# Sums over sources for ten tiles at a time, a comparison ramp in PSUM, and a prologue in another order

## The reference

```
# layer 0, with x + ... and a layer norm around it
h        = relu(concat(x[src], edge_attr) @ W1.T + b1)
agg      = segment_sum(h @ W2.T + b2, dst)            # per destination
gi, gh   = agg @ Wih.T + bih, x @ Whh.T + bhh         # a GRU cell
r, z     = sigmoid(i_r + h_r), sigmoid(i_z + h_z);  n = tanh(i_n + r * h_n)
x        = layernorm(x + (1 - z) * n + z * x)
# layer 1: a mean over edges, the other way round
agg, deg = segment_sum(x[dst], src), segment_sum(1, src)
x        = layernorm(x + (agg / max(deg, 1)) @ weight + x @ root_weight + bias)
```

## Time and profile before

| | |
|---|---|
| median of 3 runs | 5907.92 us |
| the profiled execution | 5940.19 us, its span 5938.5 us |
| mean granted TensorE clock | 0.832 |
| busy | PE 75%, PEld 64%, DVE 56%, ACT 40%, POOL 55% |
| DMA engines, data moved | 40% to 70% busy in most slices, 998.72 MB |

### The profile page before, as it was taken

One profiled execution on the slowest core, in us unless ns is written; L12 is line 12 of the kernel. 1 busy time (PEld: TensorE's weight loads), 2 busy tenths in 40 slices (PEclk: granted clock), 3 DMA queues, 4 the chain that ended last, 5 costly groups with the idle time before them and its releaser, 6 DMA issues.

```text
span 5938.5 us, 89837 instructions
## 1 busy us (share of the span) xinstructions
PE 4445.1 (75%) x30332; PEld 3789.5 (64%) x30332; DVE 3346.9 (56%) x9964; ACT 2362.5 (40%) x4278; POOL 3250.5 (55%) x3198
## 2 busy tenths in 40 slices
PE   6477777787777777777777877777777777777776
PEld 5366666676666666666666666666666667666654
DVE  5344656565556565655556565655565656565555
ACT  2144343434343434444444434343434343434343
POOL 2466555655555555556555655565555555555520
PEclk8566888787979797988888888888797988788889
DMA  6444657575756565655656565657474656565656
GB/s 182 77 128 128 198 147 199 143 202 145 203 145 194 152 189 160 183 167 173 180 162 190 156 190 148 199 154 200 141 206 144 198 153 192 160 180 163 173 148 178
DMA packets 1017763, 998.72 MB, mean 168 GB/s; under 512 B 204167, under 2 KB 857548, under 8 KB 1016921
## 3 DMA queue, kind: packets, MB, share of 16 engines
q1 hardware_dynamic: 830878, 459.88, 27.8%
q10 hardware_dynamic: 84075, 321.56, 17.1%
q0 software_dynamic: 102352, 211.43, 14.0%
HBM read 655.22 MB, written 337.22 MB: 167 GB/s over the span
## 4 chain that ended last, share of the span: by engine, by line
PE 48%; DVE 17%; another core or an unknown queue 15%; issue 10%; ACT 5%; DVEq 1%; ACTq 0%
PE stream_pse L1163 11%; PE stream_psa L1172 10%; PE stream_psw L1187 9%; PE stream_pse L1155 6%; DVE stream_col L933 5%; PE stream_psw_third L1187 5%; ACT stream_a_sb L848 3%; DVE stream_sums L943 3%; DVE stream_sums L947 2%; DVE stream_row L928 1%; ACT stream_hid L810 1%; DVE stream_yg L911 1%; DVE stream_acc L903 1%; PE stream_psw_third L1211 1%
## 5 line engine op out<-in xcount | busy, mean ns | idle before, releaser
L793 POOL DMA_INDIRECT stream_yg<-y,stream_idx x3125 | 3197.7, 1023 | 2322.7 <-ACT stream_hid L810 1446.9
L848 ACT CAST stream_a_sb<-stream_psa 98x512 f16<-98x512 f32 x3125 | 1772.3, 585 | 2996.1 <-remote 1176.4
L911 DVE TENSOR_TENSOR stream_yg<-stream_pse,stream_yg 128x384 f32<-128x384 f32 x1250 | 611.3, 489 | 1850.1 <-remote 947.1
L1172 PE MATMUL stream_psa<-stream_col,stream_row 128*98 128x256 f16 x6250 | 1292.6, 312 | 439.7 <-ACT stream_a_sb L848 221.8
L1187 PE MATMUL stream_psw<-stream_z,stream_strip 128*128 128x257 f16 x5850 | 930.9, 293 | 407.4 <-DVE stream_sums L947 345.5
L1163 PE MATMUL stream_pse<-w1b,stream_ea 128*128 128x128 f32 x6250 | 1161.7, 327 | 68.5 <-DMA stream_ea<-in_ea_blocks_dram 33.6
L1172 PEld LDWEIGHTS stream_psa<-stream_col,stream_row 128*98 128x98 f16 x6250 | 825.9, 144 | 584.7 <-issue 409.5
L1163 PEld LDWEIGHTS stream_pse<-w1b,stream_ea 128*128 128x128 f32 x6250 | 1006.0, 233 | 117.8 <-issue 91.6
L933 DVE TENSOR_TENSOR stream_col<-iota_lo,stream_twin 128x1536 f16<-128x1536 f16 x1250 | 1020.7, 817 | 0.0
L1187 PEld LDWEIGHTS stream_psw<-stream_z,stream_strip 128*128 128x128 f16 x5850 | 590.9, 104 | 565.5 <-issue 312.9
L1155 PEld LDWEIGHTS stream_pse<-stream_seg,stream_hid 128*128 128x128 f32 x6250 | 855.6, 215 | 1.3
(11 more groups left out here) (202 smaller groups left out, 2053.4 us busy)
## 6 DMA issues: line engine op xcount, KB each, us to landing
A<-stream_a_sb ACTq DMA_DIRECT2D x625, 490.0 KB
stream_strip<-A SPq DMA_DIRECT2D x1862, 160.0 KB
stream_ea<-in_ea_blocks_dram SPq DMA_DIRECT2D x625, 160.0 KB
stream_yg<-y,stream_idx POOLq DMA_INDIRECT x3125
stream_col<-A SPq DMA_DIRECT2D x84, 96.0 KB, 2.5
prologue_xt<-in_xT_dram SPq DMA_DIRECT2D x14, 448.0 KB, 4.9
y<-prologue_ysb SPq DMA_DIRECT2D x14, 448.0 KB, 2.8
stream_yg<-r SPq DMA_DIRECT2D x49, 128.0 KB, 2.5
```

The lines of the kernel that those rows point to most:

```text
L793: nc.gpsimd.indirect_dma_start(out=yg[s.c % 4][:, t, :], out_offset=None, in_=h.y, in_offset=bass.IndirectOffsetOnAxis(ap=idx[s.c // (PH / ...
L848: nc.scalar.copy(a_sb[s.c % AR][0:RW, j, :], psa[BANK[j]][0:RW, :]).then_inc(a_out, 1)
L911: V.tensor_tensor(yg[s.c % 4][:, lo:hi, :], pse[half][:, 0:(hi - lo) * D].rearrange("p (t d) -> p t d", d=D), yg[s.c % 4][:, lo:hi, :], AL ...
L1172: last = nc.tensor.matmul(psa[BANK[j]][0:RW, e * LOS:(e + 1) * LOS], row1[s.c % 2][:, 2 * j + e, :], col1[s.c % 2][:, 2 * j + e, :], start ...
```

## The change

1. **Ten tiles at a time.** The sums over sources are taken once for two phases: a unit is now 10 matmuls over 10 tiles and the same two adds. There are 9 x 98 = 882 units where there were 1764; the matmuls stay 8820. Phase 0 has no units; of the 98 units of each pair, phases 1, 3, ..., 15 take 50 and phases 2, 4, ..., 16 take 48, 2 or 3 a step; phase 17 takes the last 98 alone, 4 at k = 12 and then 5 a step.
2. **Two PSUM banks** for the units and the GRU cell in place of three. A unit waits for the unit two before it; the first of a phase now waits for r as well as z. The strip ring is 4 strips of 10 tiles, no longer 7 of 5. At the end the last 8 tiles come from one strip buffer, loaded three ahead (was six).
3. **The ramp in PSUM.** The third bank holds a copy of `iota_lo`, read as 16-bit numbers, and `rows`, `cols` and `segment_hot` read it there; the keys and the results stay in SBUF.
4. **The prologue.** Two pairs of codes are turned after each of pieces 1 to 7; the one-hots' keys are stored twice side by side, so that the innermost dimension holds two elements one step apart; counts follow pieces 3, 4, 5, 6, and the short chain pieces 8, 9 and 10; weights are loaded at piece 2. SP loads the indices and edge data of the first blocks and POOL gathers blocks 0 to 3 within the prologue, after its 49 windows. The wait for the store of the degrees moves to SP at the stream's start.
5. Some buffers are shared: xb, xtb and rb lie in tt, nn and vb, with one more wait of DVE at k = 9 for the store of r of the phase before.

```diff
-UNITS = {k: 5 for k in range(12, PH)}
-UNITS[PH - 1] = UNITS[PH - 11] = 4
...
+RS = 4
+PAIR = 2 * PT
+UT = ITER // 2 * TS
+def unit_steps(p):
+    if p == 0 or p > ITER - 1:
+        return {}
+    if p == ITER - 1:
+        first, ks = 0, [12, 12, 12, 12] + [k for k in range(13, PH) for _ in range(5)][:TS - 4]
+    elif p % 2:
+        first, ks = 0, [k for k in range(12, PH) for _ in range(3 - k % 2)]
+    else:
+        first, ks = TS * 50 // 98, [k for k in range(13, PH) for _ in range(2 + k % 2)]
...
             def unit(ph, u, first):        # PE
+                if first:
                     pe.wait_ge(z_ready, ph.n(1, 1))
-                if u == 1:
                     pe.wait_ge(r_ready, ph.n(1, 1))
...
-                if u >= 3:
-                    pe.wait_ge(unit_added, ph.n(TS, u - 1))
-                for t in range(PT):
-                    last = nc.tensor.matmul(psw[(u + 2) % 3][:, 0:XC], strip[c % RING][:, t, ...], z[0][:, t, :], ...)
+                if u >= 2:
+                    pe.wait_ge(unit_added, u)
+                for t in range(PAIR):
+                    last = nc.tensor.matmul(psw[u % 2][:, 0:XC], strip[g % RS][:, t, ...], z[g // C % 2][:, t, :], ...)
                 last.then_inc(unit_done, 1)
...
             def unit_first(u):             # DVE
+                dve.wait_ge(unit_done, u + 2)
+                V.tensor_tensor(sums[:, u % TS, :], sums[:, u % TS, :], psw[u % 2][:, 0:P + 1], ALU.add)
...
-        psw = [psw2[:, 0:512], psw2[:, 512:1024], psw_third[:]]
+        psw = [psw2[:, 0:512], psw2[:, 512:1024]]
+        ramp = psi[:, 0:LOS // 2].bitcast(fp16)
...
             def paired(n, groups):
-                return h.iota_lo[:, 0:n].rearrange("p (a b) -> p a b", b=2)...
+                return ramp[:, 0:n].rearrange("p (a b) -> p a b", b=2)...
...
             def load_strip(g, ph, to, at, n):     # SP
+                if g >= RS:
+                    sp.wait_ge(unit_done, 2 * (g - RS) + 3)
...
             # prologue, DVE
-                V.tensor_tensor(oh_hi[q % 2][:], wide(f_hi[:, part], W), tall(h.iota_lo[0:SR, 0:W], SQ), ALU.is_equal)
+                for to, key, n in ((oh_hi[q % 2], f_hi, W), (oh_lo[q % 2], f_lo, P)):
+                    V.tensor_tensor(to as [SR, SQ, n // 2, 2], key[:, part, :] as the same, iota_lo as the same, ALU.is_equal)
...
             # prologue, PE
             for k in range(1, NC):
                 y(k)
-                turn_codes(k - 1)
-                if k % 2 == 1 and 3 <= k <= 9:
-                    count((k - 3) // 2)
-            places()
+                for n in pairs_at(k):          # 2k - 2, 2k - 1
+                    turn_codes(n)
+                if 3 <= k <= 6:
+                    count(k - 3)
+                if k == 8:
+                    halves()
+                if k == 9:
+                    rows_before()
+                if k == 10:
+                    turn_first()
...
             # prologue, POOL, after the 49 windows
+            for k in range(2):
+                pool.wait_ge(y_stored[k], 16 * ((NC + 1 - k) // 2))
+            pool.wait_ge(h.idx_in[0], 16)
+            for c in range(4):
+                for t in range(BT):
+                    nc.gpsimd.indirect_dma_start(out=h.yg[c][:, t, :], ..., in_=h.y, ...)
...
             # prologue, SP: the last line goes, and stands at the stream's start
-            sp.wait_ge(deg_stored, 16)
```

More of the change, by code:

```diff
@@ L233, in pair_tiles, with pairs_at @@
             return [t for t in (2 * n, 2 * n + 1) if t < QS]
+        def pairs_at(k):
+            return [n for n in (2 * k - 2, 2 * k - 1) if 0 <= n < EP]
         def quad_tiles(q):
@@ L1015, in body @@
                         read_places(s, 4 if k is None else min(8, BLOCKS + 1 - s.c))
-                units = units_of(k) if k is not None and ph.p < ITER else []
-                ops = [(f, u) for u in units for f in (unit_first, unit_second)]
+                units = units_of(ph.p, k) if k is not None else []
                 order = []
@@ L1227, in body @@
             def body(s, k=None, ph=None):
-                units = units_of(k) if k is not None and ph.p < ITER else []
+                units = units_of(ph.p, k) if k is not None else []
+                begin = units[0] if units and k == min(STEPS[ph.p]) else None
                 def next_unit():
                     if units:
-                        unit(ph, units.pop(0))
+                        u = units.pop(0)
+                        unit(ph, u, u == begin)
                 pe.wait_ge(ea_in[s.c % 2], s.turn(2, 16))
```

255 lines of the change are left out of this document (144 added, 111 removed).

## The result

The changed kernel takes 6023.13 us (median of 4 runs, 6007.9 to 6035.79), the kernel before in the same set 5907.52 us: ratio 1.0188, 95% interval 1.0171 to 1.0205. The forecast was 5793 us. The profiled execution has a span of 6024.1 us against 5938.5.

The account below looks back on a forecast made before the run. It took PE to bound the steps with units, with a small real wait for DVE; -30 - 125 - 23 + 55 + 8 = -115 us on 5940.19 gave 5825, as a median 5793 us, own range 5660 to 5900.

Parts of the forecast that it names:

- Last section, "loads three strips ahead, 13 us: nothing": Last section: keeps its matmuls and loads three strips ahead, 13 us at its pace a pair; claimed to cost nothing.
- Phase 17, +55: Phase 17: 490 more matmuls in its 20 steps, claimed to add 55 us, bounds +20 and +93.
- "isn't late": SP's queue: the next block's edge data, behind strip loads that wait for units, claimed to come in time.
- Phases 1 to 16, -125 and +8: Steps with units: half the adds saves 0.4 us a step, -125 us; each phase's first unit waiting for r, +8 us.
- the backlog: Steps with units: PE ran 2.0 us behind its record, so some of its recorded waits for adds aren't real.
- Rival 2: Steps with units: PE is truly full, fewer adds return nothing, phase 17 pays its whole 62 us; 5925 us, chance 0.13.
- the first rival: DVE's comparisons: with the ramp in PSUM they fall to one element a cycle, +333 us; 6125 us, chance 0.14.
- the +8 us for the first unit's wait: First unit of a phase: also waits for r, up to some 0.5 us in 17 phases; range 0 to +17.
- Two banks covered by 0.6 to 0.9 us: Units in two PSUM banks: PE's other work outlasts DVE's adds by 0.6 to 0.9 us, hiding the missing third bank.
- Phase 0, -23: Phase 0: without its 490 matmuls it goes at the open blocks' pace, -23 us, bounds 0 and -62.
- Ramp in PSUM, no change: DVE's comparisons: reading the ramp from PSUM leaves their time unchanged; faster POOL gathers, perhaps 266 us, give nothing.
- Prologue, -30: Prologue: block ends 22 us sooner and the first add's wait for gathered rows saves 8; -30 us, bounds -45 and -10.

Follow-up runs that it names:

- e1: Changed kernel with strips loaded seven ahead in the last section, from separate early and late tile buffers; slow chip: 6018.43 us, 1.0124 of the kernel before.
- e2: Changed kernel with SP loading the next block's edge data ahead of the strips; slow chip: 6017.44 us, 1.0119 of the kernel before.
- e17: Changed kernel with one token add of one column a unit, leaving out layer 1's sums; slow chip, single run: 6023.68 us.
- e3: Changed kernel with the comparisons reading the ramp from SBUF again; slow chip: 6001.47 us, 1.0083 of the kernel before.
- e4: Changed kernel with five-tile units in two banks and seven strips ahead in the last section; slow chip: 6423.65 us, 1.0801 of the kernel before.
- e7: Changed kernel with one token add of one column a unit, leaving out layer 1's sums; quick chip, single run: 4680.81 us.
- e8: Changed kernel with the 20 gathers of blocks 0 to 3 moved from the prologue into the stream; quick chip, single run: 4716.12 us.
- e18: Changed kernel with seven strips ahead in the last section, edge data before strips, first gathers in the stream; slow chip: 5873.18 us, 0.9946 of the kernel before.
- e9: The kernel before, unchanged, profiled on a quick chip; single run: 4585.73 us.
- the mended kernel: Changed kernel with seven strips ahead in the last section, edge data before strips, first gathers in the stream: 0.9848 of the kernel before (quick chip), 0.9946 (slow).
- e10: The changed kernel, unchanged, on a quick chip: 4717.34 us, 1.0229 of the kernel before.

## Why the prediction was wrong, step by step

- **Last section, "loads three strips ahead, 13 us: nothing"**: the step that failed worst, +74 us. It took the look-ahead as time (three pairs of 4.5 us) and not as a place in SP's queue, where the loads stand behind the store of a finished row. The loop of 11.0 us for two pairs shows it, and e1 takes the 74 us back (with the buffers changed too). The rule stated in the prediction's own terms, what stands behind a waiting instruction, was asked for DVE and not for SP here.
- **Phase 17, +55**: measured +83.6. With the edge data first (e2) the phase takes 339.3 us, 54.6 over the 284.7 of the kernel before, so the term for the 490 matmuls was right; the failed sentence is that the edge data, behind strip loads that wait for units, "isn't late". It was, 31 us in all.
- **Phases 1 to 16, -125 and +8**: measured -36. The working took half of the adds' 5% of the chain; the paragraph before it had the backlog that spoke against it. e17: with the adds all but gone the unit steps stay at 168.5 us. Rival 2 (PE is truly full) was right on that, and its 5925 us is nearest to the result, but by a hair (98 us short, where the first rival's 6125 is 102 too high for a reason that didn't occur) and it too lacked the two queue costs. What gave the 3.9 us a phase in the unit steps isn't the ramp (e3) nor the length of the adds (e17); fewer hand-overs a step is what remains, and wasn't isolated on a slow chip. The steps before k = 13 lost 1.6 us a phase, also unexplained; the +8 us for the first unit's wait was not measured by itself.
- **Two banks covered by 0.6 to 0.9 us**: held for ten tiles (PE waits 50 us in all). e4, whose units are half as long, shows what two banks cost where nothing covers them: 836 us of waits.
- **Phase 0, -23**: right, -22.9, and for the reason given: the pace of open blocks.
- **Ramp in PSUM, no change**: right (949 ns). That the faster gathers are hidden was right on the slow chip (e3) and wrong on a quick one.
- **Prologue, -30**: measured -12, and -5 in the open blocks. The doubled keys gave what was forecast, 2.71 and 3.48 us. But `at` came at 89.3 and not 81, PE was free for windows at 107 and not 95, so the last window went at 167.2 instead of 157, and the 20 gathers ended at 193 instead of 182; the stream began at 201.7. And the prefetch itself, worked out as good for 8 us, holds the block's end: without it the first relu comes 14 us sooner (e7 against e8, quick chip; 12 us in e18).

The deviations add up: 18 - 5 + 81 + 29 + 4 + 74 = 201 us, which is 86 + 115. One sum in the prediction is off by itself: with 0 to -0.8 us a step and the prologue's bounds, its own range is 5653 to 5938 us and not 5660 to 5900. The result lies outside both.

## What to carry to other kernels

How far ahead a load is issued is a place in a queue: write down what stands before it there, and what that waits for, in the last section and in the densest phase as well as in the steady state. An engine's share of the chain is no price; where a consumer that waits for nothing else starts 2 us after its producer's recorded end, suspect the producer, and a kernel with token work in place of the suspected cost tests it in one run. Moving work from a phase in which the granted clock then falls (0.90 to 0.64 in phase 0) into one that is full is a loss by itself: 22.9 us gained there, 54.6 paid in phase 17 with the edge data first.

## What the runs showed of the hardware that was not expected

- The same kernel takes 5908 us on one chip and 4604 on another, at mean granted clocks of 0.832 and 0.893 (e9). The bound of the kernel before changes with it, from PE to POOL, and the worth of small edits with the bound: the mended kernel gains 0.5% on one and 1.5% on the other.
- A comparison of 1536 16-bit elements takes 949 ns with one operand in PSUM and 952 with both in SBUF; but the gathers that POOL issues beside it take 951 ns instead of 1049 (e3; 1023 in the kernel before) on the slow chip, and 948 (e10) instead of 1021 (e9) on a quick one. (The Trainium skill, "SBUF — State Buffer", section "SBUF: two separate sides", says that a DVE instruction with two SBUF inputs and a GpSimd instruction that reads SBUF lock one pair of ports against each other for a whole instruction. The direction agrees; that the lock is the cause is not shown.)
- A store of 49 KB in 6288 packets landed 22.6 us after it was issued and kept the DMA engines 93% busy over 24 us (kernel before).
